# Small matmuls on side-by-side tiles of the PE array, and the rotary addition moved to an accumulating DMA, in a Mamba block beside a two-layer local-attention transformer

## The reference

```python
x_c    = depthwise_conv(x_inner, conv_w)            # 4 taps, 512 channels
x_dbl  = silu(x_c + conv_b) @ x_proj_w.T            # 48 columns: 16 for dt, 16 B, 16 C
dt     = softplus(x_dbl[:, :16] @ dt_proj_w.T + b)
h_t    = exp(dt * A) * h_t-1 + dt * x * B ;  y = sum over states of h_t * C
q, k   = l2norm(q) * qs, l2norm(k) * ks
q      = q * cos * scale + rotate_half(q) * sin * scale   # k: the same, / scale
sim    = where(mask, -max, q @ k.T)
h      = layernorm(shift(x)) @ w1 + b1 ; a, g = split(h)  # 682 columns each
x      = x + (a * gelu(g)) @ w2 + b2
```

## Time and profile before

| | |
|---|---|
| median of 3 runs | 2194.63 us (2186.33 to 2199.24) |
| the profiled execution, device time | 2194.64 us |
| its span, first to last instruction | 2192.7 us |
| PE busy / DVE busy / ACT busy / POOL busy | 2033.0 / 1986.4 / 1651.2 / 946.4 us |
| granted TensorE clock, mean | 0.984 |

### The profile page before, as it was taken

The page is one execution under the profiler, slowest core; times in us unless marked ns, Lnnn a source line. Parts: engine busy times, 40 slices in busy tenths (PEclk is TensorE's granted clock), DMA queues, the critical chain, the costliest instruction groups (busy, mean ns, idle before and its releaser), DMA issues. The chain is left out here.

```text
span 2192.7 us, 37661 instructions
## 1 busy us (share of the span) xinstructions
PE 2033.0 (93%) x10944; PEld 1318.7 (60%) x10944; DVE 1986.4 (91%) x2740; ACT 1651.2 (75%) x4028; POOL 946.4 (43%) x1086
## 2 busy tenths in 40 slices
PE   6789989999999999999999999999999999998897
PEld 2456556655666566565665566665566656666565
DVE  2899989999999999999999999999999999999892
ACT  3786868868787787877878687886778878877772
POOL 2444343544434544354444543455343544443440
PEclk9899999999999999999999999999999999999998
...
GB/s 104 175 200 154 207 195 199 131 197 187 177 199 156 192 194 173 205 170 207 179 146 192 182 223 167 177 172 192 194 174 219 129 198 196 167 221 176 187 125 53
DMA packets 113130, 388.52 MB, mean 177 GB/s; under 512 B 11408, under 2 KB 32272, under 8 KB 94368
## 3 DMA queue, kind: packets, MB, share of 16 engines
q0 software_dynamic: 46080, 151.02, 37.9%
...
...
## 5 line engine op out<-in xcount | busy, mean ns | idle before, releaser
L750 DVE TENSOR_TENSOR_SCAN hb<-dA,state,hb 128x512 f32<-128x512 f32 x512 | 667.5, 1304 | 16.4 <-ACT dA L947 2.6
L1152 POOL COPY state<-hb 128x2 f32<-128x2 f32 x256 | 242.7, 948 | 391.2 <-DVE hb L750 390.2
L1168 POOL DMA_DIRECT2D ysum<-dA x256 | 221.0, 874 | 433.7 <-DVE dA L757 358.1
L947 ACT ACTIVATE dA<-dt_sb,amat 128x512 f32<-128x512 f32 x512 | 344.8, 718 | 84.0 <-DMA ysum<-dA 82.8
L1440 PE MATMUL ring<-hT,w 128*128 128x256 f32 (+1 forms) x1536 | 354.7, 388 | 11.6 <-ACT hT L1094 11.0
L1440 PEld LDWEIGHTS ring<-hT,w 128*128 128x128 f32 (+1 forms) x1536 | 272.7, 182 | 84.8 <-ACT hT L1094 20.5
L743 DVE TENSOR_TENSOR hb<-u_sb,bc 128x1024 f32<-128x1024 f32 x256 | 308.4, 1205 | 10.2 <-DMA bc<-bc_rows 7.9
L757 DVE TENSOR_TENSOR dA<-hb,bc 128x1024 f32<-128x1024 f32 x256 | 314.2, 1227 | 0.0
L1048 ACT ACTIVATE rot<-rot,rnorm 128x64 f32<-128x64 f32 x1024 | 254.6, 342 | 49.9 <-POOL rnorm L1237 49.7
L1073 ACT ACTIVATE probs<-ring,nmax 128x256 f32<-128x256 f32 x512 | 235.2, 476 | 73.7 <-DVE nmax L832 73.3
L1237 POOL TENSOR_TENSOR rnorm<-rnorm,powers 128x8 f32<-128x8 f32 x128 | 234.6, 1833 | 24.4 <-POOL rnorm L1234 24.0
...
## 6 DMA issues: line engine op xcount, KB each, us to landing
bc<-bc_rows SPq DMA_DIRECT2D x128, 1024.0 KB, 5.9
ysum<-dA POOLq DMA_DIRECT2D x256, 512.0 KB, 7.1
...
w<-in_w SPq DMA_DIRECT2D x16, 768.0 KB, 13.1
...
ysum<-xconv POOLq DMA_DIRECT2D x32, 256.0 KB, 4.4
```

What stands on the lines that cost most here:

```text
L750: dve.tensor_tensor_scan(hb[:, k % H_RING, :], dA[:, k % DA_RING, :], hb[:, k % H_RING, :], state[:, k:k + 1], ALU.mult, ALU.add).then_inc ...
L947: act.activation(dA[:, k % DA_RING, :], dt_sb[:, j, :], ACT.Exp, scale=amat[:, n:n + 1]).then_inc(dA_ready.sem, 1)
L1152: pool.tensor_copy(state[:, 2 * m:2 * m + 2], hb[:, slot:slot + 2, T - 1]).then_inc(state_saved.sem, 1)
```

## The change

**Tiles of the array.** `convolve` takes two blocks `j` at once and cuts each 128x128 diagonal into 64x64: four matmuls of 512 columns for each tap, one on each quarter of the array, over two banks. The input projection's rows are permuted on the host (`crossed`) so that the quarters put each channel in its place. `x_dbl` does 256 tokens on the left half of the array and 256 on the right. `dt_proj` takes two blocks at once, on the rows 32 to 47 and 96 to 111; the second pair waits until the first is done (`dt_crossed`). The mask is laid down by four 64x64 matmuls instead of two full ones. The last block of `hidden` is padded to 64 columns, and its two windows of 128 tokens lie on the two halves of the array and so on 128 partitions of the result; ACT and DVE handle it as 128x128 instead of 42x256. The last matmul of `feed_out` reads all 128 rows, against two versions of the last weight block with zeros in the other window's half; `w1` and `w2` are larger by the padding (1408 and 896 KB for a layer).

**The rotary addition.** L827 is taken out of DVE's order. POOL issues a DMA from `sq` to `rot` with addition, 256 KB, for each q and k (`add_rotated`, stage `rot`, 16 in a chunk). `norm_heads` and the next `square` of the same operand wait for its landing.

**Orders.** All orders are rewritten. No stage of DVE, ACT or SP is added or dropped, POOL has the 16 `rot`, PE has two `conv` and two `dt` instead of four each. The count of switches between ACT's function tables in the written orders goes from 145 to 148 for the whole run.

The order strings are shown for the middle passes of ACT and POOL, with the old lines only around `q(4)`; the setup of constants is left out.

```diff
 ACT_ORDER = """
...
-+dA ++in(0) ++in(1) +x2T(0) +dA +skip(1) +dA ++in(2) +dA +dA ++in(3) +q(4) +k(4) +dA +dA +turn(q,4)
-+turn(k,4) +dA +dA +hn(1) ++silu(0) ++silu(1) +hT(1) +heads(4) +q(5) +dA +dA +dA +h(1,0) +h(1,1) +h(1,2)
...
++dA v(7) heads(7) +dA +q(0) e(7,0) e(7,1) +k(0) pT(7,0) e(7,2) e(7,3) pT(7,1) rb(7) pT(7,2) pT(7,3) +dA +dA
++dA +v(0) +turn(q,0) +turn(k,0) +heads(0) hn(3) +q(1) hT(3) +e(0,0) +e(0,1) +dA +dA +dA +e(0,2) +e(0,3)
+h(3,0) h(3,1) +dt(2) +k(1) +dt(3) +dA +dA h(3,2) h(3,3) h(3,4) h(3,5) +dA +dA +turn(q,1) +dA +dA last(3)
++turn(k,1) +pT(0,0) +rb(0) +heads(1) +dA +dA +dA +dA +pT(0,1) +z(0) +pT(0,2) +q(2) +start(0) +start(1) +z(1)
++z(2) +k(2) +dA +dA +pT(0,3) +e(1,0) +e(1,1) +e(1,2) +e(1,3) +pT(1,0) +pT(1,1) +v(1) +turn(q,2) +dA +pT(1,2)
++pT(1,3) +turn(k,2) +rb(1) +z(3) +heads(2) +v(2) +q(3) +dA +dA +dA +dA +e(2,0) +e(2,1) +e(2,2) +last(0)
++e(2,3) +k(3) +pT(2,0) +pT(2,1) +dA +pT(2,2) +hn(0) +dA ++xn(0) +pT(2,3) +hT(0) +v(3) +dA +h(0,0) +h(0,1)
++turn(q,3) +h(0,2) +h(0,3) +turn(k,3) +h(0,4) +h(0,5) +dA +heads(3) +dA ++xn(1) ++xnT(0) +rb(2) +e(3,0)
++e(3,1) +dA +dA +dA +dA ++xnT(1) +e(3,2) +e(3,3) +pT(3,0) +pT(3,1) +dA ++in(0) +x2T(0) +pT(3,2) +pT(3,3) +dA
++q(4) +k(4) +dA +rb(3) ++in(1) +skip(1) +dA ++in(2) ++in(3) +dA +dA +turn(q,4) +turn(k,4) +dA +hn(1)
+++silu(0) ++silu(1) +q(5) +hT(1) +k(5) +heads(4) +dA +last(1) +dA +dA +h(1,0) +h(1,1) +h(1,2) +h(1,3)
++h(1,4) +h(1,5) +dA +dA +turn(q,5) +turn(k,5) +e(4,0) +e(4,1) +dA +dA +e(4,2) +e(4,3) ++xdbl +v(4) +pT(4,0)
++heads(5) +pT(4,1) +dA +dA +pT(4,2) +pT(4,3) +dA ++dt(0) ++dt(1) +x2T(1) +e(5,0) +e(5,1) +q(6) +rb(4)
++e(5,2) +e(5,3) +k(6) +dA +dA +rb(5) +dA +dA +dA +pT(5,0) +pT(5,1) +v(5) +pT(5,2) +pT(5,3) +dA +dA
++turn(q,6) +turn(k,6) +heads(6) +v(6) +q(7) +hn(2) +k(7) +hT(2) +e(6,0) +e(6,1) +e(6,2) +e(6,3) +dA +dA +dA
++pT(6,0) +dA +h(2,0) +h(2,1) +h(2,2) +h(2,3) +h(2,4) +h(2,5) +last(2) +pT(6,1) ++dA +rb(6) +turn(q,7)
++turn(k,7) +pT(6,2) +pT(6,3) ++dA ++skip(0)
 """
 POOL_ORDER = """
...
+add(30) scan +scan add(31) +turn(q,0) +rot(q,0) +rot(k,0) +add(0) merge(1) +turn(k,0) +q(1) +add(1) +scan
+stats(3) +skip(0) +scan +rot(q,1) +scan +add(2) +add(3) +scan +rot(k,1) +turn(q,1) +turn(k,1) +scan +add(4)
++add(5) +q(2) +scan +scan +add(6) +scan +add(7) +add(8) +rot(q,2) +rot(k,2) ++halo +scan +turn(q,2) +q(3)
++turn(k,2) +scan +add(9) ++norm(0) ++norm(1) +add(10) +turn(q,3) +stats(0) +rot(q,3) +add(11) +scan
++rot(k,3) +q(4) +carry +scan +scan +turn(k,3) +add(12) +scan +add(13) +add(14) +add(15) +scan +scan +add(16)
++add(17) +scan +rot(q,4) +rot(k,4) +scan +turn(q,4) +skip(1) +turn(k,4) +stats(1) +q(5) +scan +scan +add(18)
++add(19) +rot(q,5) +rot(k,5) +scan +add(20) +turn(q,5) ++tail +add(21) +turn(k,5) +merge(0) +q(6) +add(22)
++scan +scan +scan +add(23) +add(24) +add(25) +scan +rot(q,6) +rot(k,6) +scan +turn(q,6) +scan +q(7)
++turn(k,6) +add(26) +add(27) +stats(2) +turn(q,7) +turn(k,7) +rot(q,7) +scan +rot(k,7) +add(28) +add(29)
++scan +scan +carry2 ++q(0)
 """
...
-    rot_ready = Signal("rot_ready", 2 * NA)
+    rot_added = [Signal(f"rot_added_{x}", D16 * NA, primed=0) for x in "qk"]
...
                 sp.sem_inc(passed, 1)
-                sp.dma_start(scratch[it % 2, :, :], xdbl[0:2 * STATES, :]).then_inc(bc_stored.sem, D16)
+                for v in range(2):
+                    sp.dma_start(scratch[it % 2, :, v * T // 2:(v + 1) * T // 2], xdbl[v * XPAD:v * XPAD + 2 * STATES, :])\
+                      .then_inc(bc_stored.sem, D16)
...
                 dve.tensor_tensor(sq[:, i, :].rearrange("p (h d) -> p h d", d=DH), src, cos, ALU.mult)\
                    .then_inc(rotary_ready.sem, 1)
-                dve.wait_ge(*sine_ready.at(it, n + 1))
-                dve.wait_ge(*rotary_ready.at(it, n + 1))
-                dve.tensor_tensor(rot[:, i, :], rot[:, i, :], sq[:, i, :], ALU.add).then_inc(rot_ready.sem, 1)
...
                 l = f // 2
-                rows = P if i < NH - 1 else LAST
+                n = 2 * WIN if i < NH - 1 else WIN
                 dve.wait_ge(*filled(it, ("h", f, i)))
                 dve.wait_ge(*gelu_ready.at(it, f * NH + i + 1))
                 b1a = C_B1A + l * NH + i
-                dve.scalar_tensor_tensor(hid[0:rows, i, :], bank(it, ("h", f, i))[0:rows, 0:2 * WIN],
-                                         par[0:rows, b1a:b1a + 1], gel[0:rows, i % 2, :], ALU.add, ALU.mult)\
+                dve.scalar_tensor_tensor(hid[:, i, 0:n], bank(it, ("h", f, i))[:, 0:n],
+                                         par[:, b1a:b1a + 1], gel[:, i % 2, 0:n], ALU.add, ALU.mult)\
                    .then_inc(hid_ready.sem, 1)
 
             def add_feed(f):
...
             def square(i, name, a):
                 n = 2 * a + i
-                act.wait_ge(*rot_ready.at(it, n - 1))
+                if it or a:
+                    act.wait_ge(*rot_added[i].at(it, D16 * a))
                 act.wait_ge(*filled(it, (name, a)))
                 act.activation(sq[:, i, :], bank(it, (name, a))[:, :], ACT.Square).then_inc(sq_ready.sem, 1)
...
                 n = 2 * a + i
-                act.wait_ge(*rot_ready.at(it, n + 1))
+                act.wait_ge(*rot_added[i].at(it, D16 * (a + 1)))
...
+            def add_rotated(name, a):
+
+                i = "qk".index(name)
+                n = 2 * a + i
+                pool.wait_ge(*sine_ready.at(it, n + 1))
+                pool.wait_ge(*rotary_ready.at(it, n + 1))
+                pool.sem_inc(passed, 1)
+                pool.dma_start(rot[:, i, :], sq[:, i, :], accum_op=ALU.add).then_inc(rot_added[i].sem, D16)
+
...
-            def convolve(j):
-                pe.wait_ge(*xin_ready.at(it, j + 1))
+            def convolve(half):
+
+                j0 = 2 * half
+                pe.wait_ge(*xin_ready.at(it, j0 + 2))
                 pe.wait_ge(*halo_ready.at(it, 1))
-                pe.wait_ge(*freed(it, ("conv", j)))
+                pe.wait_ge(*freed(it, ("conv", j0)))
+                pe.wait_ge(*freed(it, ("conv", j0 + 1)))
                 for k in range(TAPS):
-                    m = pe.matmul(bank(it, ("conv", j))[:, :], convd[:, j * TAPS + k, :], xin[:, j, k:k + T],
-                                  start=(k == 0), stop=(k == TAPS - 1))
-                m.then_inc(*done(it, ("conv", j)))
+                    for c in range(2):
+                        for r in range(2):
+                            rows = slice(r * DH, (r + 1) * DH)
+                            m = pe.matmul(bank(it, ("conv", j0 + r))[c * DH:(c + 1) * DH, :],
+                                          convd[rows, (j0 + c) * TAPS + k, :], xin[rows, j0 + c, k:k + T],
+                                          start=(k == 0), stop=(k == TAPS - 1), skip_group_check=True)
+                            if k == TAPS - 1 and c == 1:
+                                m.then_inc(*done(it, ("conv", j0 + r)))
 
             def x_dbl():
                 pe.wait_ge(*freed(it, ("xdbl",)))
                 for j in range(NJ):
                     pe.wait_ge(*xconv_ready.at(it, j + 1))
-                    m = pe.matmul(bank(it, ("xdbl",))[0:XROWS, :], xpw[:, j, :], xconv[:, j, :],
-                                  start=(j == 0), stop=(j == NJ - 1))
+                    for v in range(2):
+                        m = pe.matmul(bank(it, ("xdbl",))[v * XPAD:(v + 1) * XPAD, 0:T // 2], xpw[:, j, :],
+                                      xconv[:, j, v * T // 2:(v + 1) * T // 2], start=(j == 0), stop=(j == NJ - 1),
+                                      skip_group_check=True)
                 m.then_inc(*done(it, ("xdbl",)))
 
-            def dt_proj(j):
+            def dt_proj(half):
+
                 pe.wait_ge(*xdbl_ready.at(it, 1))
-                pe.wait_ge(*freed(it, ("dt", j)))
-                pe.matmul(bank(it, ("dt", j))[:, :], dtw[2 * STATES:XROWS, j * P:(j + 1) * P],
-                          xdbl[2 * STATES:XROWS, :], start=True, stop=True).then_inc(*done(it, ("dt", j)))
+                for j in (2 * half, 2 * half + 1):
+                    pe.wait_ge(*freed(it, ("dt", j)))
+                for turn in range(2):
+                    if turn:
+                        pe.wait_ge(*dt_crossed.at(it, half + 1))
+                    for odd in range(2):
+                        j, v = 2 * half + odd, turn ^ odd
+                        rows = slice(v * XPAD + 2 * STATES, v * XPAD + XROWS)
+                        m = pe.matmul(bank(it, ("dt", j))[:, v * T // 2:(v + 1) * T // 2], dtw[rows, j * P:(j + 1) * P],
+                                      xdbl[rows, :], start=True, stop=True)
+                        if turn:
+                            m.then_inc(*done(it, ("dt", j)))
+                        elif odd:
+                            m.then_inc(dt_crossed.sem, 1)
...
-                msk = mask0[:, :] if it == 0 and w == 0 else mask[:, w % 2, :]
+                first = 2 * WIN if it == 0 and w == 0 else w % 2 * WIN
                 for p in (2 * c, 2 * c + 1):
```

(41 more changed lines are left out.)

393 lines of the change are left out of this document (188 added, 205 removed).

## The result

The changed kernel takes 2177.9 us (median) against 2194.9 us for the kernel before in the same comparison: the ratio is 0.9934, 95% interval 0.9918 to 0.9949. So it is 17 us faster, where 92 us were forecast. The time lies in the range and the direction is right, but four fifths of the gain are missing. The profiled execution has a span of 2176.2 us.

A forecast was written before the change was run, and what follows sets the result against it. PE and DVE together were taken as the limit. DVE's 106 us less gave 2087, PE's 136 less gave 2057; the later counts, plus 14 give-back and 1.9 outside the span: 2103 us, whole range 2065 to 2190.

The forecast's parts named there:

- the SP and DMA step: SP's loads and DMA engines: one more store and 0.3 MB a chunk count as nothing; the additions raise DMA share to 0.86.
- DVE, 106 us: DVE's saving: 102.4 us from L827 with the time in front of it, 4 us from the last hidden block.
- PE, 136 us: PE's saving: 17 us a chunk from convolution, `x_dbl`, `dt_proj`, last hidden block, `feed_out` and mask, 136 us in all.
- Give-back, 14 us: ACT's waits for `ysum` landings grow by half, 41 us, and a third of that, 14 us, reaches DVE.
- The coupling of the two engines: DVE and PE share the limit, and both must get shorter for the kernel to get shorter.
- pairs only: Rival on PE: quarters run only in pairs, convolution and mask save nothing; time 2125, chance 0.12.
- both landings rivals: DMA engines give the gain back (2151, chance 0.16); late `rot` landings on ACT's path make it slower (2236, chance 0.11).
- their signs: Signs of a wrong forecast: ACT waiting for `rot<-sq` by 50 us and more, or for `ysum` over 160 us.
- the second: Rival: the DMA engines give the gain back as landings of the additions go from 4.4 to 7.1 us; 2151, chance 0.16.
- The new orders lose as much in waits as the engines save: Rival of no change: the new orders lose in waits 1 us in 20 of each chunk; time 2190, chance 0.06.
- The sign named for it: DVE idle for much more than 220 us with none of the other signs would put the orders at fault.
- The chunk: A steady chunk was taken as 252 us, with PE busy for 242.8 and DVE for 238.3; eight chunks were counted.

The follow-up runs named there:

- e_sp: Changed kernel with SP's order mended: `bc(5)` ahead of `++x(0) ++x(1) +w2(0)`; `xres(0)`, `wol(1)` ahead of `bc(11)`; `w1(1)` between `bc(12)` and `bc(13)`: 2103.2 us.
- e_sp_dve: Changed kernel with the mended SP order, but the rotation's addition back on DVE and no additions issued by POOL: 2173.3 us, ratio 0.9909.
- e_sp_conv: Changed kernel with the mended SP order, but the convolution as 32 matmuls of 128 x 128 weights a chunk instead of 64 on quarters: 2144.6 us.
- e_small: Changed kernel with its own orders, each of the 128 rotary DMA additions moving 4 of 512 columns only: 2147.9 us, ratio 0.9788.
- e_tail: Changed kernel with the mended SP order, and in PE's tail `+out(0)` ahead of `+hT(3)` instead of behind `+h(3,3)`: 2096.2 us, ratio 0.9552.

## Why the prediction was off

- **The step that failed is the SP and DMA step.** It says "SP issues one store more a chunk and `w1` and `w2` are 172 KB larger a layer ... nothing beside some 46 MB". I counted bytes and not places. The change lays out SP's order anew: `bc(5)` went behind `++x(1)` and `w2(0)`. `bc(14)` had the weights in front of it already, but DVE's new order comes to it 10.3 us after its issue instead of 15.5. Whose landing is late was asked for `ysum` and `rot` alone. `bc`, which DVE waits for directly, has no term in the sum. Its wait rose from 7.9 to 62.0 us; with the four stages moved it is 6.2 and the time 2103.2. That this is the forecast's 2103 to the microsecond is luck: DVE saved 11 us less busy time than forecast, PE 20 less, and the give-back was not there.
- **DVE, 106 us:** L827 is gone with its 88.7 us and the 13.7 in front. The busy time fell by 81.4 where 92.7 were forecast; L755 took 15.7 us more (308.4 to 324.1), beside POOL's multiplication, and the scans 8.2 less (667.5 to 659.3). The multiplication met DVE in the kernel before too, more on the scans; the new orders moved the meetings, and I had no term for that. The last hidden block gave its 4 us (15.0 to 11.0).
- **PE, 136 us:** the prices were right or cautious. From start to start the convolution takes 7.03 us a chunk (forecast 7.1), hidden's last block 1.02 (1.02), `feed_out` 5.18 (5.28), `x_dbl` 1.88 (1.96), a pair of `dt_proj` 1.40 (1.35). The mask's busy time fell by 25 us (78.2 to 53.2), where I had 13. But PE's busy time fell by 86.9 only, since the clock went down at the stalls: 24.3 us in five chunks, seen when e_sp took the stalls away. I had held the clock at 0.99. In e_sp it is 1917.2, so 115.8 below the kernel before; why not the whole 136 was not followed up. The Trainium skill ("TensorEngine Tiling (Array Packing)", section "Tiling Modes") says that changing the mode drains the engine. The trace shows that what this costs here is small: the quads take 7.03 us for 16 steps of 0.43, 0.15 over them.
- **Give-back, 14 us, from ACT's waits for `ysum`:** the sign was wrong, they fell from 82.8 to 32.7. The DMA share was near (0.83, 0.85 in e_sp, for 0.86). Landings of `rot` are 4.7 us in the median for the 4.4 taken; ACT waited 39.2 us for them, more than the 20 allowed, and 20.1 us in e_sp.
- **The coupling of the two engines** was right: e_sp_dve and e_sp_conv show that both parts were needed. Of the rivals, pairs only is out (7.1 us), and so are both landings rivals as they were named: no wait for `rot` or `ysum` reached their signs. Yet the second was near the truth: the DMA engines did give the gain back, through `bc` and SP's order, and with the new orders the additions' transfers had some 30 us of it (e_small). "The new orders lose as much in waits as the engines save" had 0.06, because "nothing in the rows asks for it"; the two SP orders side by side would have asked for it at `bc(5)`. The sign named for it, DVE idle for much more than 220 us, is what came (271).
- **The chunk.** I took the stretch of 252 us in the earlier trace rows for a chunk; the period is 262.5, so PE idled for 11 of it and not 9. And I counted eight equal chunks: the last one with the tail took 315.4 us before, 314.8 after and 318.6 in e_sp. PE is busy there for 271 of 315 us, and of these edits only e_tail's made it shorter.
